# A third expansion buffer with a lead of two slots, superslots over a layer's first 345 slots, and copies of counts first in ScalarE's turn

## The reference, cut to what matters

```python
q, k, v = x @ Wq + bq, x @ Wk + bk, x @ Wv + bv      # [3125, 64]
e = edge_attr @ We                                   # [100000, 64]
kj = k[src] + e
alpha = sum(q[dst] * kj, -1) / sqrt(64)
p = exp(alpha - segment_max(alpha, dst)[dst])
w = p / segment_sum(p, dst)[dst]
x = segment_sum((v[src] + e) * w[:, None], dst) + x @ Ws + bs
x = relu(x)                                          # and a layer norm after layers 0 and 1
```

## Time and profile before

| | us |
|---|---|
| median of 3 runs | 4713.49 (4710.97 to 4714.2) |
| profiled execution | 4721.57 |
| its span in the profile | 4719.8 |
| loop of layer 0: first gather starts, last addition starts | 95.9, 1237.15 |
| loop of layer 1, first gather starts | 1276.3 |
| loop of layer 2: first gather starts, last addition starts | 2457.2, 3593.30 |
| busy: PE, DVE, ACT, POOL | 3468.1, 3236.7, 2427.2, 2503.7 |

### The profile page before, as it was taken

The page is one execution under the profiler, slowest core; times in us unless marked ns, Lnnn a source line. Parts: engine busy times, 40 slices in busy tenths (PEclk is TensorE's granted clock), DMA queues, the critical chain, the costliest instruction groups (busy, mean ns, idle before and its releaser), DMA issues. The chain is left out here.

```text
span 4719.8 us, 91070 instructions
## 1 busy us (share of the span) xinstructions
PE 3468.1 (73%) x24128; PEld 3020.2 (64%) x24128; DVE 3236.7 (69%) x10293; ACT 2427.2 (51%) x8514; POOL 2503.7 (53%) x2592
## 2 busy tenths in 40 slices
PE   3767666666667776666656777777775799996789
PEld 2556555555555555555555766767675799996788
DVE  7677767677657777677764777778785433354998
ACT  0766666666275766666627666656542100000555
POOL 5777777676277777777617777777752100000000
PEclk9687888888667878888866888888875899997555
DMA  3344444444143444444414444444423200000000
GB/s 78 100 101 104 106 113 122 113 121 110 51 99 96 109 103 115 114 120 121 111 49 98 103 105 104 104 99 108 101 63 105 94 2 2 2 1 1 2 3 3
DMA packets 576845, 384.28 MB, mean 81 GB/s; under 512 B 421913, under 2 KB 498833, under 8 KB 576343
## 3 DMA queue, kind: packets, MB, share of 16 engines
q1 hardware_dynamic: 373463, 151.17, 12.5%
q0 software_dynamic: 81344, 84.68, 9.8%
q10 hardware_dynamic: 121536, 142.57, 9.8%
HBM read 312.87 MB, written 65.24 MB: 80 GB/s over the span
## 5 line engine op out<-in xcount | busy, mean ns | idle before, releaser
L617 POOL DMA_INDIRECT arena<-node_table,arena x1660 | 1601.7, 965 | 604.4 <-issue 474.0
L772 PE MATMUL ps<-arena 128*128 128x129 f32 x4980 | 943.9, 320 | 187.1 <-DVE arena L922 103.0
L681 ACT ACTIVATE arena<-arena 128x129 f32<-128x129 f32 x2490 | 742.7, 300 | 451.2 <-DVE arena L890 443.9
L772 PEld LDWEIGHTS ps<-arena 128*128 128x128 f32 x4980 | 788.0, 225 | 274.0 <-DVE arena L922 138.0
L919 DVE TENSOR_SCALAR arena<-arena 128x128 f32<-128x128 uint16 x2490 | 883.3, 361 | 88.7 <-PE ps L772 37.8
L617 POOL DMA_INDIRECT arena<-last_node_table,arena x830 | 793.2, 956 | 281.6 <-issue 235.3
L890 DVE TENSOR_TENSOR arena<-ps,arena 128x258 f32<-128x258 f32 x1245 | 524.7, 421 | 591.2 <-PE ps L761 244.8
L1208 PE MATMUL ps<-arena 128*128 128x192 bf16 x6875 | 587.0, 247 | 12.7 <-DVEq L1368 4.9
L1208 PEld LDWEIGHTS ps<-arena 128*128 128x128 bf16 x6875 | 584.7, 98 | 14.6 <-issue 7.4
L761 PE MATMUL ps<-arena 128*128 x2496 | 503.4, 335 | 106.1 <-ACT e L671 37.6
L761 PE MATMUL ps<-arena,e 128*128 x2484 | 494.6, 331 | 110.5 <-DVE arena L890 52.2
(11 more groups left out here) (338 smaller groups left out, 4625.5 us busy)
## 6 DMA issues: line engine op xcount, KB each, us to landing
arena<-in_attr SPq DMA_DIRECT2D x1245, 96.0 KB, 2.2
arena<-slot_rows ACTq DMA_DIRECT2D x249, 320.0 KB
edge_counts<-al ACTq DMA_DIRECT2D x397, 100.0 KB
arena<-node_table,arena POOLq DMA_INDIRECT x1660
edge_counts<-stage ACTq DMA_DIRECT2D x198, 100.0 KB
arena<-last_node_table,arena POOLq DMA_INDIRECT x830
arena<-edge_counts SPq DMA_DIRECT2D x24, 500.0 KB
stage<-edge_counts SPq DMA_DIRECT2D x16, 500.0 KB
```

The source lines that it names most:

```text
L617: pool.indirect_dma_start(out=RING[:, t % R_SLOTS, XO:XO + XG], out_offset=None, in_=table[:, :], in_offset=bass.IndirectOffsetOnAxis(ap=I ...
L681: ins = act.activation(PR[j % 3][:, q], PR[j % 3][:, q], ACT.Copy, accum_out=AL[w % 2][:, c:c + 1])
L772: ins = pe.matmul(BPS[j % 2][:, 0:AB], WOH[j % 2][:, q], RING[:, r + q, D32:D32 + AB], start=q == 0, stop=q == BT - 1)
```

## The change

It does four things. The superslots of layers 0 and 1 are spread over 345 slots instead of 411, with weight 1 for a slot up to 196 and 2 beyond, and those of layer 2 evenly over 345: 97, 148 and none in the three stretches named above (59, 46 and none in layer 2), again at most one per slot. UPS gets a third buffer at PSUM column 2560, and the expansion runs two slots ahead: two are made before the loop, and the expansion of slot j waits for the product of slot j - 3. In ACT's turn the copy comes first, then the one-hots, then the store, then the sums. DVE's product reads the buffer j % 3.

```diff
 def adjacency_slots(l, j):
 
-    light, last = 196, NBAT - 4
-    weigh = lambda k: 36 * min(k, light) + 100 * max(0, k - light) if l < 2 else k
+    light, last = 196, NBAT - 70
+    weigh = lambda k: min(k, light) + 2 * max(0, k - light) if l < 2 else k
     return share_weighed(ADJ_N[l], weigh(min(j, last)), weigh(min(j + 1, last)), weigh(last))
...
-            UPS = [ps[:, 512 * k:512 * k + BT * AB] for k in range(2)]
+            UPS = [ps[:, o:o + BT * AB] for o in (0, 512, 2560)]
...
                             for j in ja:
+                                for k in adjacency_slots(l, j - 2) if j >= 2 else ():
+                                    copy_counts(k)
+                                if j + 4 < NBAT:
+                                    one_hot_rows(j + 4)
                                 for k in adjacency_slots(l, j - 3) if j >= 3 else ():
                                     store_counts(k)
-                                if j + 4 < NBAT:
-                                    one_hot_rows(j + 4)
-                                for k in adjacency_slots(l, j - 2) if j >= 2 else ():
-                                    copy_counts(k)
                                 sum_products(j)
...
                         pe.wait_ge(s["oht"], j + 1)
-                        if j >= 2:
-                            pe.wait_ge(s["pr"], j - 1)
+                        if j >= 3:
+                            pe.wait_ge(s["pr"], j - 2)
                         for q in range(BT):
-                            ins = pe.matmul(UPS[j % 2][:, q * AB:(q + 1) * AB], OHT[j % 6][:, q * P:(q + 1) * P],
+                            ins = pe.matmul(UPS[j % 3][:, q * AB:(q + 1) * AB], OHT[j % 6][:, q * P:(q + 1) * P],
...
-                    expand(0, block_of(0))
+                    for j in range(2):
+                        expand(j, block_of(j))
                     for w in range(NWIN + 1):
                         for ja, jb in steps(w):
                             for j in ja:
-                                if j + 1 < NBAT:
-                                    expand(j + 1, block_of(j + 1))
+                                if j + 2 < NBAT:
+                                    expand(j + 2, block_of(j + 2))
...
-                        dve.tensor_tensor(PR[j % 3], UPS[j % 2].rearrange("p (a b) -> p a b", b=AB),
+                        dve.tensor_tensor(PR[j % 3], UPS[j % 3].rearrange("p (a b) -> p a b", b=AB),
```

## The result

The changed kernel takes 4741.4 us (median of four, 4737.7 to 4746.1) against 4713.8 for the one before: ratio 1.0056, 95% interval 1.0041 to 1.0070. It is slower by 27 us where 119 us less was forecast. The profiled execution took 4746.1 us, with a span of 4744.3.

A forecast was written before the change was run, and what follows sets the result against it. GpSimd's gather stream and what follows it were taken to bound each layer; 35 us (full ring) + 2 x 36 (ends of the first two layers) + 12 (last layer) = 119 off 4713.5 gave 4595, range 4565 to 4668.

The forecast's parts named there:

- what bounds a layer: A layer is GpSimd's gather stream, 2.50 us a slot or 1037 us a layer, and what follows the last gather.
- The end of a layer: Windows 8 to 10 without superslots: the wait after the last gather falls by 36 us in each of the first two layers.
- In the last layer the end: Last layer's end without its 17 superslots: 12 us less, bounds 0 and 18.
- I cost the move at nothing, with the lead as its cover: ACT's turn: moving the copy ahead of store and one-hots makes the store 0.95 us later and costs nothing.
- the circle now spans four slots instead of two, so it leaves the path: Heavy stretch: the round from product through sums, one-hots, copy and superslot matmuls to the expansion no longer sets the pace.
- the circle isn't what sets the pace: Rival: a heavy window costs 130 us, 44 us lost on the ring waits, 4673 us in all; chance 0.12.
- the sum of busy times as proof that 148 superslots fit in slots 196 to 344: Heavy window: busy times plus softmax idle come to 100 us at most, under the gathers' 112.4 us.
- The full ring: GpSimd's waits for aggregations when products fall ten slots behind: 39 us in layers 0 and 1, of which 35 go.
- Slower: stores in every slot: Rival: from slot 196 each store waits for the previous landing; at 3.2 us a slot 34 us slower, 4748; chance 0.04.
- Gathers held by DVE: Rival: each superslot holds a gather for its whole 1.08 us, 13 us a layer, 4623 us in all; chance 0.05.

The follow-up runs named there:

- e4: The changed kernel with ACT's old order (store, one-hots, copy, sums), lead and spread kept: 4691.7 us.
- e3: The kernel before with only ACT's turn changed, to copy, one-hots, store, sums: 4787.5 us, ratio 1.0156.
- e1: The kernel before with only the third buffer and the lead of two slots added: 4720.2 us, ratio 1.0014.
- e10: e6 without the lead and third buffer, ACT's turn one-hots, copy, sums: 4618.5 us, ratio 0.9803.
- e6: The changed kernel with the stores and their register loads issued by SP, ACT's turn copy, one-hots, sums: 4613.4 us, ratio 0.9794.
- e2: The kernel before with only the superslots' new spread over 345 slots: 4679.6 us, ratio 0.9932.
- e12: The changed kernel with ACT's turn copy, store, one-hots, sums and superslots of layers 0 and 1 spread evenly over 345 slots: 4656.1 us.
- e5: The changed kernel with the loads of the one-hots' rows issued by SP instead of ACT: 4718.6 us, ratio 0.9999.
- e11: e6 with the superslots of layers 0 and 1 spread evenly over 345 slots: 4620.5 us, ratio 0.9813.

## Why the prediction was wrong

**Right: what bounds a layer, and its end.** The gather stream plus what follows it is the layer, before and after. The end of a layer came as worked out in windows 9 and 10 (33 and 17 us), 78.5 us less in all where 84 was taken; window 8 took 56.7 us where at most 54 was taken. In the last layer the end gave 3.6 us instead of 12; with the same superslots the runs show anything from 69 to 98 us for it, and what moves it stays open.

**Wrong: "I cost the move at nothing, with the lead as its cover".** This step failed, in ACT's turn. Moving the store behind the one-hots costs 50 us with lead and spread (e4) and 72 us by itself (e3). The step looked at what is queued behind the waiting store, only the sums, and not at what is queued ahead of it, under which issue and wait are hidden. It also took 11.1 us for the landing wait where four lines add to 31.1, and left out the register load, which moved with the store. From e4 to the changed kernel ACT's idle time grows by 47.7 us: 26.9 under "issue", 9.7 at register loads, 10.2 at landings, 0.9 elsewhere.

**Wrong: "the circle now spans four slots instead of two, so it leaves the path".** It left the path and freed nothing (e1, e10). The circle was read off two waits; that both are long because they stand behind ACT's turn fits e6, where nothing but ACT's queue was relieved, but wasn't tried on the kernel before. The rival "the circle isn't what sets the pace" had this right and gave it 0.12, with 4673 us; with the old order that is roughly what e2 and e4 show (4680 and 4692).

**Wrong: the sum of busy times as proof that 148 superslots fit in slots 196 to 344.** DVE and ACT were about as busy as reckoned (window 5 got six superslots more, not seven), but a turn holds the store's waits too, and with a store in nearly every slot there is no empty turn to make them up. The full ring was forecast to fall from 39 to 4 us. It rose to 83 with the old order (e4) and to 125 with the new one. At 106 superslots instead of 148 it is 16 (e12), and with the stores on SP 15 (e6).

**The rival that came true** is "Slower: stores in every slot", with 0.04: 4748 us for a slot of 3.2 us, and a turning point near 3.1. The measured slot is 3.11 us after 2.76. The two streams grew by 46.8 and 57.1 us, where it had 59. Its mechanism was right in place and price, but about half of its cause is the order (ring waits 82.7 us in e4, 125.3 in the changed kernel), which it didn't name. That the price came out so near is in part luck.

**Gathers held by DVE** was a rival on its own and turned out a small part: the mean gather in the light stretch went from 0.976 to 0.988 us, and summed over layers 0 and 1 the gathers beyond 0.944 us grew from 34.6 to 52.1 us.

## What to carry to other kernels

In an engine's hand-written order, a DMA issue that has to wait was cheaper here behind instructions already queued than behind a chain in which the engine waits for itself. Where another queue runs ahead, give it the store with all that belongs to it, the loads of its registers too. A wait in the profile names who came last, not who sets the pace: before a buffer or a lead is built to shorten it, ask what its releaser waited for. "Issue" in a list of waits can hide a few long pieces among many short ones: look at the longest. And a sum of busy times under the bound shows only that the work fits, not that the waits between do.

## What the runs showed of the hardware that was not expected

A row load of 320 KB delays the landing of a 100 KB store issued up to 2.3 us after it, in whichever queue the two stand. Such stores took 3.2 to 3.7 us from issue to landing on average in all fourteen kernels, and the others 1.95 to 2.10 (650 to 1000 and 1900 to 2300 us). That holds with both on ACT (3.49 us in the changed kernel), with the load on SP (3.72, e5) and with the store on SP (3.19, e6).

A load of 17 registers (L93) keeps ACT's queue for 3.64 us in the median of the six in 650 to 1000 us. With the sums behind it, ACT stood still for 3.84 us.

Gathers get longer where many of the superslots' DVE instructions come together with the counting of sources, and hardly where they come alone. Over the first 196 slots of layers 0 and 1 the mean is 0.972 and 0.976 us before, with 60 superslots, 0.973 to 0.988 in the nine kernels with 97, and 1.011 to 1.037 in e11 and e12 with 139. From slot 196 to 344, without sources, it is 0.953 and 0.958 us before, with 128 superslots, and 0.957 to 0.971 in the nine kernels with 148. In the last layer, which counts no sources, the gathers' sum beyond 0.944 us is 10 to 12 us for 830 gathers in before, changed, e6, e11 and e12 alike. The Trainium skill, SBUF — State Buffer, "Who interferes with whom", says that a VectorE instruction in a two-port mode and GpSimd lock each other out of a shared port for the whole instruction. The traces agree that DVE's work lengthens GpSimd's gathers, but not that each instruction does so by its whole length; which of DVE's instructions it is was not tried, nor why e12's gathers are longer than e11's.
